# Self-attention inside a six-stage transformer program: score tiles of 32x64, one exponential per pair of batches, another order of the work around them

## The chip, the cores and the metric

The kernel is one program on one core of a Trainium2 chip. The metric is the device time of a run in microseconds (us). Three runs of the kernel before took 3310.77, 3310.79 and 3312.28 us; the median is 3310.79 us. "Within 0.2%" is 6.6 us of that.

## The reference

The input x is 8 batches of 64 rows of 512 features (512 rows in all). Six layers follow one another, each as x = x + layer(layernorm(x)): a cross attention with a GRU, a state space block, a convolution with attention and eight dense experts (stage 3), a cross attention over 1601 rows (stage 4), a causal self-attention with rotations (stage 5), and eight routed experts (stage 6). The change concerns the self-attention of stages 3 and 5, each over 64 rows of one batch, 16 heads of 32 features:

```python
# stage 3 (inside _L0_ffn_ref), after the convolution
scores = jnp.einsum('bhqd,bhkd->bhqk', q, k) / jnp.sqrt(jnp.float32(dh))
attn = jax.nn.softmax(scores, axis=-1)
ctx = jnp.einsum('bhqk,bhkd->bhqd', attn, v)
# stage 5 (_L1_attn_ref)
q = apply_rope(q, cos, sin)
k = apply_rope(k, cos, sin)
scores = jnp.einsum('bqhd,bkhd->bhqk', q, k) * SCALE
scores = jnp.where(causal[None, None], -1e+30, scores)
attn = jax.nn.softmax(scores, axis=-1)
out = jnp.einsum('bhqk,bkhd->bqhd', attn, v).reshape(B, S, D)
```

## The kernel before

Everything is FP32. Activations lie with features on 128 partitions: a tile [128, 4, 512] holds 4 chunks of 128 features (index c or g) by 512 rows. A chunk g holds four heads, head a of it on partitions 32a to 32a+31. Each engine has its own program, written by hand, and these programs meet through semaphores: `at.step(name)` counts, `wait_ge(*at.done(name))` waits. PSUM `PS` has eight banks of 512 columns; `bank_reader[k]` is the name of the step that last read bank k, and TensorE waits for it before it writes the bank again.

The attention (`attn_pe`, `attn_act`, `attn_dve`, `attn_pool`) works in four pairs of batches (`bp`, `NBP` = 4, 128 rows). For a pair:

- Scores (L1183): one matmul per chunk g gives all four heads at once, 128 query rows by 4 x 128 key columns. For this the keys are copied into a block-diagonal tile `KBD` (zero outside a head's 32 partitions), the first pair by VectorE (L1244, 4 copies), the other pairs by GpSimd (L1172). Half of the 128x128 scores of a head are between different batches and are masked away.
- `maxima` on VectorE, for each half q of 8 heads: scale and mask (L1253, 128x1024), maximum (L1257), sign (L1259).
- `exps` on ScalarE: 16 activations of 128x128 with a bias and an accumulated sum (L1225).
- Normalise on VectorE, for each half: reciprocal (L1271), multiply (L1273, 128x1024).
- `values` on TensorE: 16 transposes of the probabilities (L1195, T below) into banks 4 to 6, copied out by ScalarE (L1235), then 16 matmuls of 128x32 stationary values (L1204, O below) into bank 7, copied out by VectorE (`out`, L1263).

The order on VectorE is written out: maxima(0), maxima(1), then for bp = 0 to 3: normalise(bp), and from bp = 1 on out(bp-1) and maxima(bp+1). On TensorE: scores(0), scores(1), then values(bp) and scores(bp+2).

Ahead of it, in stage 3, come the linears for q, k (L296) and v (L1289, bias added by VectorE at L1297). In stage 5 come q, k, then four plus four rotation matmuls (L1796), each followed by three VectorE operations (L1802, L1803, L1805), then the v linear. After it comes the output linear (L296), the next norm and the experts. Both stages pass a mask tile.

Of the kernel before, what the change touches and what calls it, by code (L numbers as in the profile page):

```python
# [142 lines left out]
def build(nc, marks, new, t, stages=(1, 2, 3, 4, 5, 6)):  # L143
    ctx = ExitStack()
    with ctx:
# [71 lines left out]
        def bank(k, n=512):  # L217
            return PS[:, k, 0:n]
# [932 lines left out]
        KBD = [RB4[0], RB4[1]]  # L1151

# [3 lines left out]
        least = [misc[:, 0:H], misc[:, 16:16 + H]]  # L1156
# [3 lines left out]
        HALF_H = H // 2  # L1160

        def attn_pool(pool, at, tag, K, ready):
            for x in KBD:
                pool.memset(x[:, :, :], 0.0).then_inc(*at.step(f"{tag}.zero"))
            pool.wait_ge(*at.own())
            for due in at.last(*ready):
                pool.wait_ge(*due)
            for bp in range(1, NBP):
                if bp >= 2:
                    pool.wait_ge(*at.done(f"{tag}.S{bp - 2}"))  # L1170
                for a in range(G):
                    pool.tensor_copy(KBD[bp % 2][a * HD:(a + 1) * HD, :, a * P:(a + 1) * P],  # L1172
                                        K[a * HD:(a + 1) * HD, :, bp * P:(bp + 1) * P]).then_inc(*at.step(f"{tag}.kb{bp}"))

        def attn_pe(pe, at, tag, Q, V, ready):
            def scores(bp):
                pe.wait_ge(*at.done(f"{tag}.kb{bp}"))
                for g in range(KC):
                    if bp:
                        pe.wait_ge(*at.done(f"{tag}.masked{bp - 1}.{g // 2}"))  # L1180
                    elif bank_reader.get(g):
                        pe.wait_ge(*at.done(bank_reader[g]))
                    mm = pe.matmul(bank(g), Q[:, g, bp * P:(bp + 1) * P], KBD[bp % 2][:, g, :], start=True, stop=True)  # L1183
                    if g % 2:
                        mm.then_inc(*at.step(f"{tag}.S{bp}.{g // 2}"))
                at.same(f"{tag}.S{bp}")

            def values(bp):
                for g in range(KC):
                    pe.wait_ge(*at.done(f"{tag}.p{bp}.{g // 2}"))  # L1190
                    k = 4 + g % 3
# [5 lines left out]
                    bank_reader[k] = f"{tag}.T{bp}.{g}.out"
                if bank_reader.get(7):
                    pe.wait_ge(*at.done(bank_reader[7]))
                for g in range(KC):  # L1200
                    pe.wait_ge(*at.done(f"{tag}.T{bp}.{g}.out"))
                    for a in range(G):
                        h = G * g + a
                        mm = pe.matmul(PS[a * HD:(a + 1) * HD, 7, g * P:(g + 1) * P], V[:, bp, h * HD:(h + 1) * HD],  # L1204
                                          probsT[:, h, :], start=True, stop=True)
                mm.then_inc(*at.step(f"{tag}.O{bp}"))
                bank_reader[7] = f"{tag}.O{bp}.out"

            for due in at.last(*ready):
                pe.wait_ge(*due)  # L1210
            scores(0)
            scores(1)
            for bp in range(NBP):
                values(bp)
                if bp + 2 < NBP:
                    scores(bp + 2)
            for g in range(KC):
                bank_reader[g] = f"{tag}.masked{NBP - 1}.1"

        def attn_act(act, at, tag):  # L1220
            def exps(bp):
                for h in range(H):
                    if h % HALF_H == 0:
                        act.wait_ge(*at.done(f"{tag}.least{bp}.{h // HALF_H}"))
                    act.activation(probs[bp % 2][:, h, :], probs[bp % 2][:, h, :], ACT.Exp, bias=least[bp % 2][:, h:h + 1],  # L1225
                                   accum_out=sums[bp % 2][:, h:h + 1]).then_inc(*at.step(f"{tag}.exp{bp}.{h // HALF_H}"))
# [3 lines left out]
            for bp in range(NBP):  # L1230
                for g in range(KC):
                    act.wait_ge(*at.done(f"{tag}.T{bp}.{g}"))
                    if bp:
                        act.wait_ge(*at.done(f"{tag}.O{bp - 1}"))
                    act.activation(PT[:, g, :], bank(4 + g % 3), ACT.Copy).then_inc(*at.step(f"{tag}.T{bp}.{g}.out"))  # L1235
                if bp and bp + 1 < NBP:
                    exps(bp + 1)

        def attn_dve(dve, at, tag, K, ready, O, mask):
            dve.wait_ge(*at.done(f"{tag}.zero"))  # L1240
            for due in at.last(*ready):
                dve.wait_ge(*due)
            for a in range(G):
                dve.tensor_copy(KBD[0][a * HD:(a + 1) * HD, :, a * P:(a + 1) * P],  # L1244
                                K[a * HD:(a + 1) * HD, :, 0:P]).then_inc(*at.step(f"{tag}.kb0"))

            def maxima(bp):
                if bp >= 2:
                    dve.wait_ge(*at.done(f"{tag}.T{bp - 2}.3"))
                for q in (0, 1):  # L1250
                    dve.wait_ge(*at.done(f"{tag}.S{bp}.{q}"))
                    x, m = probs[bp % 2][:, q * HALF_H:(q + 1) * HALF_H, :], least[bp % 2][:, q * HALF_H:(q + 1) * HALF_H]
                    dve.scalar_tensor_tensor(out=x, in0=PS[:, 2 * q:2 * q + 2, :].rearrange("p g (a k) -> p (g a) k", k=P),  # L1253
                                                 scalar=HD ** -0.5, in1=mask.unsqueeze(1).broadcast_to([P, HALF_H, P]),
                                                 op0=ALU.mult, op1=ALU.add).then_inc(*at.step(f"{tag}.masked{bp}.{q}"))
# [3 lines left out]
                    dve.tensor_scalar(m, m, -1.0, None, ALU.mult).then_inc(*at.step(f"{tag}.least{bp}.{q}"))  # L1259
# [919 lines left out]
```

## Time and profile before

| what | value |
|---|---|
| median of three runs | 3310.79 us |
| profiled execution, its own time | 3310.42 us |
| its span in the trace | 3308.6 us |
| mean granted TensorE clock | 0.949 |
| busy: PE, DVE, ACT, POOL | 89%, 40%, 31%, 8% of the span |
| attention of stage 3, first scores to last output copy | about 1141 to 1192 us |
| attention of stage 5, the same | about 3017 to 3070 us |

A duration of a matmul record includes its way through the array, so records overlap: the step from one to the next is shorter than a record. A row of the timeline gives start, length, what it is, and in brackets how long the engine idled before and what ended that.

### The profile page before, as it was taken

To read this page: it belongs to the slowest core of one execution; us is meant where nothing else is said; L and a number is where in the kernel's file an instruction comes from. 1 tells how busy PE (TensorE), PEld (TensorE's weight loads), DVE (VectorE), ACT (ScalarE), POOL (GpSimd) and SP (SyncE) were. 2 spreads that over 40 slices of the span, in tenths; PEclk is the share of its full clock that TensorE was granted. 3 is DMA by queue.
4 is the path that set the end of the run, shared out by engine and by line. 5 is a ranking of instruction groups with operands and counts; after the bars stand their busy time and mean duration, and the time that the engine had idled before them with its cause. 6 is when DMAs were issued, how large, how long until landed. Compare 5 with 4: busy or idle time off the path is not lost.

```text
span 3308.6 us, 35885 instructions
## 1 busy us (share of the span) xinstructions
PE 2950.1 (89%) x14622; PEld 2016.9 (61%) x14622; DVE 1337.6 (40%) x2005; ACT 1025.8 (31%) x1717; POOL 268.0 (8%) x274
## 2 busy tenths in 40 slices
PE   7766889888878879999999988999999999988787
PEld 3324537345555347888888857778777877844432
DVE  3435454454842243333333352442443344245211
ACT  3223212224331234433434322422332333233200
POOL 1110120122010000000000002011011101000000
PEclk9887999999889978999999999999999999998899
DMA  8663693861011002222222221001100100021097
GB/s 358 263 241 130 241 412 122 352 267 72 1 52 63 38 13 102 101 93 97 101 89 101 93 78 42 23 20 42 42 23 20 42 23 20 23 108 39 26 419 304
DMA packets 62267, 388.74 MB, mean 117 GB/s; under 512 B 5696, under 2 KB 12096, under 8 KB 32704
## 3 DMA queue, kind: packets, MB, share of 16 engines
q1 hardware_dynamic: 26640, 190.57, 15.2%
q0 software_dynamic: 29024, 192.23, 14.8%
q10 hardware_dynamic: 6480, 4.20, 0.4%
q8 instruction: 91, 1.49, 0.2%
q14 instruction: 32, 0.26, 0.0%
HBM read 381.72 MB, written 5.24 MB: 117 GB/s over the span
## 4 chain that ended last, share of the span: by engine, by line
PE 76%; DVE 7%; DMA 6%; ACT 5%; issue 4%; POOL 2%; SPq 0%; DVEq 0%; POOLq 0%; ACTq 0%
PE PS L373 10%; PE PS L375 10%; PE PS L374 10%; PE PS L544 4%; PE PS L296 4%; PE PS L1571 4%; PE PS L519 3%; PE PS L1552 3%; PE PS L1535 3%; PE PS L1554 3%; PE PS L1553 3%; PE PS L1537 3%; PE PS L1536 3%; DMA PR<-in_ctxN 3%; DMA ring<-in_experts 2%
## 5 line engine op out<-in xcount | busy, mean ns | idle before, releaser
L373 PE MATMUL PS<-X_high,W_high 128*128 128x512 f32 x576 | 226.1, 392 | 27.6 <-POOL W_part L1029 27.6
L374 PE MATMUL PS<-X_low,W_high 128*128 128x512 f32 x576 | 225.6, 392 | 0.0
L375 PE MATMUL PS<-X_high,W_part 128*128 128x512 f32 x576 | 225.5, 391 | 0.0
L375 PE MATMUL PS<-H_high,W_part 128*128 128x512 f32 x576 | 224.4, 390 | 0.0
L374 PE MATMUL PS<-H_low,W_high 128*128 128x512 f32 x576 | 224.4, 390 | 0.0
L373 PE MATMUL PS<-H_high,W_high 128*128 128x512 f32 x576 | 224.4, 390 | 0.0
L1037 DVE TENSOR_TENSOR W_part<-ring,W_high 128x2048 fp32r<-128x2048 f32 x63 | 147.0, 2334 | 188.6 <-ACT W_high L1004 188.6
L1004 ACT ACTIVATE W_high<-ring 128x2048 fp32r<-128x2048 f32 x72 | 136.9, 1914 | 255.0 <-PE PS L375 255.0
L1735 DVE TENSOR_TENSOR RB<-PS,rows 128x512 f32<-128x512 f32 x104 | 71.9, 691 | 307.2 <-PE PS L1554 307.2
L1043 DVE TENSOR_TENSOR H_low<-T,H_high 128x512 fp32r<-128x512 f32 x144 | 99.7, 692 | 221.2 <-ACT H_high L1024 221.2
L1535 PE MATMUL PS<-C_high,W_part 128*128 128x384 f32 (+2 forms) x512 | 177.7, 347 | 4.9 <-DVE W_part L1707 4.9
L1665 ACT ACTIVATE RC<-PS,vec 128x384 f32<-128x384 f32 (+2 forms) x128 | 76.2, 595 | 326.9 <-PE PS L1537 326.9
L1537 PE MATMUL PS<-C_high,W_part 128*128 128x384 f32 (+2 forms) x512 | 176.5, 345 | 0.0
L1536 PE MATMUL PS<-C_low,W_part 128*128 128x384 f32 (+2 forms) x512 | 176.5, 345 | 0.0
L544 PE MATMUL PS<-RC,PTs 128*64 128x512 f32 x312 | 144.7, 622 | 31.1 <-DVE PTs L871 23.4
L1552 PE MATMUL PS<-W_part,C_high 128*128 128x512 f32 x416 | 164.9, 396 | 0.0
L1553 PE MATMUL PS<-W_part,C_high 128*128 128x512 f32 x416 | 162.3, 390 | 0.0
L1554 PE MATMUL PS<-W_part,C_low 128*128 128x512 f32 x416 | 162.3, 390 | 0.0
L519 PE MATMUL PS<-RA,PR 128*64 128x448 f32 (+1 forms) x384 | 145.3, 538 | 18.5 <-DMA RB<-in_ctxT 8.2
L1023 ACT ACTIVATE T<-PS,vec 128x512 f32<-128x512 f32 x144 | 99.2, 689 | 197.1 <-PE PS L375 187.4
L296 PE MATMUL PS<-T,ring 128*128 128x512 f32 x288 | 135.4, 633 | 20.9 <-DVE T L363 10.0
L519 PE MATMUL PS<-RB,PR 128*64 128x448 f32 (+1 forms) x384 | 145.5, 539 | 0.0
(314 smaller groups left out, 5804.4 us busy)
## 6 DMA issues: line engine op xcount, KB each, us to landing
ring<-in_experts SPq DMA_DIRECT2D x96, 1024.0 KB, 4.8
ring<-in_tiles SPq DMA_DIRECT2D x39, 1024.0 KB, 4.8
RA<-in_ctxT POOLq DMA_DIRECT2D x20, 1792.0 KB, 8.9
RA<-in_ctxT POOLq DMA_DIRECT2D x20, 1536.0 KB, 6.9
T<-in_ctxN POOLq DMA_DIRECT2D x24, 1024.0 KB, 13.7
RA<-in_experts SPq DMA_DIRECT2D x24, 1024.0 KB, 12.4
RC<-in_ctxN POOLq DMA_DIRECT2D x12, 1792.0 KB, 12.7
RB<-in_ctxT POOLq DMA_DIRECT2D x12, 1792.0 KB, 13.4
```

Of the source, the lines that this page charges most:

```text
L296: mm = pe.matmul(bank(k), wt(w)[:, c, oc * P:(oc + 1) * P], x[:, c, :], start=(a == 0 and c == 0), stop=(a == len(terms) - 1 and c == KC - 1))
L373: pe.matmul(ps, a, xh, start=start, stop=False)
L374: pe.matmul(ps, a, xl, start=False, stop=False)
L375: return pe.matmul(ps, b, xh, start=False, stop=stop)
L519: mm = pe.matmul(PS[u * S:(u + 1) * S, 2 * h + j, 0:w], QP[:, c, u * S:(u + 1) * S], CT1[u][h][:, c, j * w:(j + 1) * w], start=(c == 0), s ...
L544: mm = pe.matmul(PS[u * S:(u + 1) * S, 6, :], A_[:, m, u * S:(u + 1) * S], cn(u, m), start=(m == 0), stop=(m == MT - 1))
L1535: pe.matmul(bank(n % 4, w), wkh[:, c, f], CH[h][:, c, m], start=(c == 0), stop=False)
L1536: pe.matmul(bank(n % 4, w), wkh[:, c, f], CL[h][:, c, m], start=False, stop=False)
L1537: mm = pe.matmul(bank(n % 4, w), wkl[:, c, f], CH[h][:, c, m], start=False, stop=(c == KC - 1))
L1552: pe.matmul(bank(k), CH[h][:, c, m], wvh[:, c, :], start=(c == 0), stop=False)
L1553: pe.matmul(bank(k), CH[h][:, c, m], wvl[:, c, :], start=False, stop=False)
L1554: mm = pe.matmul(bank(k), CL[h][:, c, m], wvh[:, c, :], start=False, stop=(c == KC - 1))
```

## The change

Scores become 32 matmuls per pair, one for each head and each of the two batches (32 contraction rows, 64 query columns stationary, 64 key columns moving), written to bank a, columns 64g on. No block-diagonal keys are needed. `KBD` and its copies go; GpSimd now zeroes the two probability tiles instead, whose off-diagonal 64x64 blocks stay zero. Exponentials are taken in place in `raw5` (128 x 16 x 64) by one activation per pair; the maximum is subtracted by VectorE before, the sum is reduced by VectorE after. Stage 3 has no mask any more.

```diff
+        def scores_pe(pe, at, tag, Q, K, bp):
+            if bp:
+                pe.wait_ge(*at.done(f"{tag}.raw{bp - 1}"))
...
             for g in range(KC):
+                for a in range(G):
+                    r = slice(a * HD, (a + 1) * HD)
+                    for u in (0, 1):
+                        m = slice((2 * bp + u) * S, (2 * bp + u + 1) * S)
+                        mm = pe.matmul(PS[u * S:(u + 1) * S, a, g * S:(g + 1) * S], Q[r, g, m], K[r, g, m], start=True, stop=True)
+            mm.then_inc(*at.step(f"{tag}.S{bp}"))
...
+                act.wait_ge(*at.done(f"{tag}.sub{bp}"))
+                act.activation(raw5[bp % 2], raw5[bp % 2], ACT.Exp, scale=HD ** -0.5).then_inc(*at.step(f"{tag}.exp{bp}"))
...
             def maxima(bp):
...
+                if mask:
+                    dve.tensor_tensor(x.rearrange("p (a g) k -> p a (g k)", a=G), PS[:, 0:G, 0:KC * S],
+                                      causal.rearrange("p g k -> p (g k)").unsqueeze(1).broadcast_to([P, G, KC * S]), ALU.add).then_inc(*at.step(f"{tag}.raw{bp}"))
                     dve.wait_ge(*at.own())
                     dve.tensor_reduce(m, x, AX.X, ALU.max).then_inc(*at.step())
                     dve.wait_ge(*at.own())
+                    dve.tensor_tensor(x, x, m.unsqueeze(2).broadcast_to([P, H, S]), ALU.subtract).then_inc(*at.step(f"{tag}.sub{bp}"))
+                    return
+                dve.tensor_reduce(m.rearrange("p (a g) -> p a g", a=G), ps, AX.X, ALU.max).then_inc(*at.step())
+                dve.wait_ge(*at.own())
+                dve.tensor_tensor(x.rearrange("p (a g) k -> p a g k", a=G), ps,
+                                  m.rearrange("p (a g) -> p a g", a=G).unsqueeze(3).broadcast_to([P, G, KC, S]), ALU.subtract).then_inc(*at.step(f"{tag}.sub{bp}"))
+                at.same(f"{tag}.raw{bp}", f"{tag}.sub{bp}")
+
+            def normalise(bp):
+                x, sm = raw5[bp % 2], sums[bp % 2]
+                dve.wait_ge(*at.done(f"{tag}.exp{bp}"))
+                dve.tensor_reduce(sm, x, AX.X, ALU.add).then_inc(*at.step())
+                dve.wait_ge(*at.own())
+                dve.reciprocal(sm, sm).then_inc(*at.step())
...
+                for u in (0, 1):
+                    r = slice(u * S, (u + 1) * S)
+                    dve.tensor_tensor(probs[bp % 2][r, :, r], x[r, :, :], sm[r, :].unsqueeze(2).broadcast_to([S, H, S]), ALU.mult).then_inc(*at.step(f"{tag}.p{bp}"))
...
             maxima(0)
+            values(0, 2)
             maxima(1)
+            values(2, 4)
             for bp in range(NBP):
...
+                normalise(bp)
                 if bp:
                     out(bp - 1)
-                    if bp + 1 < NBP:
-                        maxima(bp + 1)
+                if bp + 2 < NBP:
+                    maxima(bp + 2)
             out(NBP - 1)
...
+            scores_pe(pe, at, "s3.at", Q3, K3, 0)
+            values_pe(pe, at, "s3.v", "s3.wv", X3, (4, 5, 6, 7), range(0, 2))
+            scores_pe(pe, at, "s3.at", Q3, K3, 1)
+            values_pe(pe, at, "s3.v", "s3.wv", X3, (4, 5, 6, 7), range(2, 4))
...
+            for c in range(KC):
+                linear_pe(pe, at, "s5.k", [("s5.wk", N5)], (4 + c,), (c,))
+                rotate_pe(pe, at, "s5.qr", Q5, "s5.q", (c,), 0)
+            for c in range(KC):
+                rotate_pe(pe, at, "s5.kr", K5, "s5.k", (c,), 4)
+                values_pe(pe, at, "s5.v", "s5.wv", N5, (0, 1, 2, 3), range(c, c + 1))
```

TensorE waits for `p{bp}` of both halves before the first transpose of a pair. In the kernel after, `values_of(bp)` stands for `values(bp)`, and `values(a, b)` inside `attn_dve` adds the bias to the v linear's tiles a to b-1 (in stage 5 they are all added ahead of the attention).

TensorE in stage 3, from the v linear to the last pair. T holds q, k, v; sq is the identity; RC and RA hold the two probability tiles. Before:

```order
L1289 MATMUL PS<-ring,T 128x512 x16
L1183 MATMUL PS<-RB,T 128x512 x8
L1195 MATMUL PS<-sq,RC 128x128 x16
L1204 MATMUL PS<-RC,T 32x128 x16
L1183 MATMUL PS<-RB,T 128x512 x4
L1195 MATMUL PS<-sq,RA 128x128 x16
```

With the change:

```order
L1179 MATMUL PS<-T 64x64 x32
L1282 MATMUL PS<-ring,T 128x512 x8
L1179 MATMUL PS<-T 64x64 x32
L1282 MATMUL PS<-ring,T 128x512 x8
L1192 MATMUL PS<-sq,RC 128x128 x16
L1201 MATMUL PS<-RC,T 32x128 x16
L1179 MATMUL PS<-T 64x64 x32
L1192 MATMUL PS<-sq,RA 128x128 x16
```

Both first score groups moved ahead of or between the v linear's tiles; a score group is 32 small matmuls where it was four.

VectorE in the same stage, from the first reciprocal on (RB holds `raw5` in the change). Before:

```order
L1271 RECIPROCAL misc<-misc 128x8
L1273 TENSOR_TENSOR RC<-RC,misc 128x1024
L1271 RECIPROCAL misc<-misc 128x8
L1273 TENSOR_TENSOR RC<-RC,misc 128x1024
L1271 RECIPROCAL misc<-misc 128x8
L1273 TENSOR_TENSOR RA<-RA,misc 128x1024
L1271 RECIPROCAL misc<-misc 128x8
L1273 TENSOR_TENSOR RA<-RA,misc 128x1024
L1263 COPY T<-PS 128x4x128
L1253 SCALAR_TENSOR_TENSOR RC<-PS,sq 128x1024
```

With the change:

```order
L1245 TENSOR_REDUCE misc<-RB 128x16
L1247 RECIPROCAL misc<-misc 128x16
L1255 TENSOR_TENSOR RC<-RB,misc 64x16x64 x2
L1236 TENSOR_REDUCE misc<-PS 128x16
L1238 TENSOR_TENSOR RB<-PS,misc 128x1024
L1245 TENSOR_REDUCE misc<-RB 128x16
L1247 RECIPROCAL misc<-misc 128x16
L1255 TENSOR_TENSOR RA<-RB,misc 64x16x64 x2
L1259 COPY T<-PS 128x4x128
L1236 TENSOR_REDUCE misc<-PS 128x16
```

The maxima of pair 2 (L1236, which read the scores of pair 2 from PSUM) now stand between the normalisation of pair 0 and that of pair 1; before, pair 1 was normalised first. Stage 5 has the same order with L1229, L1232 and L1234 in place of L1236 and L1238.

## Rows read from the trace of the kernel before

**Rows 1.** The page, busy time of each engine

```profile
PE 2950.1 (89%) x14622; PEld 2016.9 (61%) x14622; DVE 1337.6 (40%) x2005; ACT 1025.8 (31%) x1717; POOL 268.0 (8%) x274
```

**Rows 2.** Chain of waits in order of time, stage 5: start, length, what

```profile
3017.51 3.60 PE PS L1183 x4
3024.21 6.26 ACT RC L1225 x32
```

**Rows 3.** Timeline of PE, stage 3 attention: start, length, what, idle before

```profile
1155.74 2.82 PE L1195 MATMUL PS<-sq,RC 128*128 128x128 f32 x12 [6.03 <-DVE RC L1273]
1159.64 1.09 PE L1195 MATMUL PS<-sq,RC 128*128 128x128 f32 x4 [1.07 <-ACT RC L1235]
1160.66 1.94 PE L1204 MATMUL PS<-RC,T 128*32 128x128 f32 x32
1162.52 4.39 PE L1183 MATMUL PS<-RB,T 128*128 128x512 f32 x8
1166.75 2.01 PE L1195 MATMUL PS<-sq,RA 128*128 128x128 f32 x16
1168.68 1.25 PE L1204 MATMUL PS<-RC,T 128*32 128x128 f32 x32
1169.86 3.70 PE L1183 MATMUL PS<-RB,T 128*128 128x512 f32 x8
1185.03 1.97 PE L1195 MATMUL PS<-sq,RA 128*128 128x128 f32 x8 [4.47 <-DVE RA L1273]
```

**Rows 4.** Timeline of ACT and PE, stage 3, end of k and the v linear

```profile
1124.97 13.90 PE L1289 MATMUL PS<-ring,T 128*128 128x512 f32 x32
...
1125.18 0.69 ACT L1408 ACTIVATE T<-PS,vec 128x512 f32<-128x512 f32 x1 [2.75 <-PE PS L296]
```

**Rows 5.** Timeline of DVE, stage 3

```profile
1138.91 0.69 DVE L1297 TENSOR_TENSOR T<-PS,rows 128x512 f32<-128x512 f32 x1 [2.74 <-PE PS L1289]
...
1144.78 1.22 DVE L1257 TENSOR_REDUCE misc<-RC 128x8 f32<-128x1024 f32 x1
...
1154.23 0.20 DVE L1271 RECIPROCAL misc<-misc 128x8 f32<-128x8 f32 x1
1154.46 1.22 DVE L1273 TENSOR_TENSOR RC<-RC,misc 128x1024 f32<-128x1024 f32 x1
...
1191.74 0.69 DVE L1263 COPY T<-PS 128x512 f32<-128x512 f32 x1 [3.09 <-PE PS L1204]
```

**Rows 6.** Timeline of PE and DVE, stage 5: rotations, v linear, first transposes, last copy

```profile
3001.11 13.90 PE L1289 MATMUL PS<-ring,T 128*128 128x512 f32 x32
3033.36 2.82 PE L1195 MATMUL PS<-sq,RC 128*128 128x128 f32 x12 [6.03 <-DVE RC L1273]
...
3010.17 0.69 DVE L1805 TENSOR_TENSOR T<-T 128x512 f32<-128x512 f32 x1
...
3069.14 0.69 DVE L1263 COPY T<-PS 128x512 f32<-128x512 f32 x1 [3.02 <-PE PS L1204]
```

**Rows 7.** Windows: stretch, its length, PE, PEld, DVE, ACT, POOL busy, clock, DMA

```profile
1156.00:1163.00 7.00, 5.93 (x49) 4.75 (x49) 4.17 (x6) 5.05 (x20) 0.00 (x0) 0.50 0.01 2
1163.00:1170.00 7.00, 7.00 (x57) 4.00 (x57) 4.95 (x6) 2.62 (x8) 0.00 (x0) 0.93 0.00 1
...
1185.00:1192.00 7.00, 5.53 (x48) 4.45 (x48) 2.28 (x4) 5.10 (x14) 0.00 (x0) 0.55 0.00 0
...
3033.00:3040.00 7.00, 5.57 (x48) 4.53 (x48) 4.40 (x7) 5.66 (x24) 0.00 (x0) 0.50 0.00 0
```

**Rows 8.** Small tiles: matmuls and weight loads, timeline; L1204's forms, ns min/median/max

```profile
L1204 PE MATMUL PS<-RC,T x256: 272/421/424, 1160.7 to 3068.8; 128*32 128x128 f32 x128
...
2894.66 1.09 PE L1602 MATMUL PS<-PTs,RB 128*64 128x128 f32 x16
...
1168.68 0.59 PEld L1204 LDWEIGHTS PS<-RC,T 128*32 128x32 f32 x24 [0.17 <-issue]
...
2888.83 0.20 PEld L1571 LDWEIGHTS PS<-RC,T 32*64 32x64 f32 x8 [0.35 <-issue]
```

More of the change, by code:

```diff
@@ L1159, in build @@
         NBP = T // P
[L1160 to L1191, printed above, removed]
+        def attn_pool(pool, at, tag):
+            for k, x in enumerate(probs):
+                pool.memset(x, 0.0).then_inc(*at.step(f"{tag}.zero{k}"))
@@ L1197, in values @@
[L1197 to L1205, printed above, removed]
@@ new lines, in scores_pe, with values_of @@
+            mm.then_inc(*at.step(f"{tag}.S{bp}"))
+            if bp == NBP - 1:
+                bank_reader.update({k: f"{tag}.raw{bp}" for k in range(G)})
+        def values_of(pe, at, tag, V, bp):
+            for g in range(KC):
+                if g == 0:
+                    pe.wait_ge(*at.done(f"{tag}.p{bp}"))
+                k = 4 + g % 3
+                if bank_reader.get(k):
+                    pe.wait_ge(*at.done(bank_reader[k]))
+                for a in range(G):
+                    mm = pe.transpose(PS[:, k, a * P:(a + 1) * P], probs[bp % 2][:, G * a + g, :], C["ident"])
+                mm.then_inc(*at.step(f"{tag}.T{bp}.{g}"))
+                bank_reader[k] = f"{tag}.T{bp}.{g}.out"
+            if bank_reader.get(7):
+                pe.wait_ge(*at.done(bank_reader[7]))
+            for g in range(KC):
+                pe.wait_ge(*at.done(f"{tag}.T{bp}.{g}.out"))
+                for a in range(G):
+                    h = G * g + a
+                    mm = pe.matmul(PS[a * HD:(a + 1) * HD, 7, g * P:(g + 1) * P], V[:, bp, h * HD:(h + 1) * HD],
+                                      probsT[:, h, :], start=True, stop=True)
+            mm.then_inc(*at.step(f"{tag}.O{bp}"))
+            bank_reader[7] = f"{tag}.O{bp}.out"
@@ L1235, in attn_act, with attn_dve @@
                     act.activation(PT[:, g, :], bank(4 + g % 3), ACT.Copy).then_inc(*at.step(f"{tag}.T{bp}.{g}.out"))
[L1236 to L1245, printed above, removed]
-            def maxima(bp):
[L1248 to L1255, printed above, removed]
+                if bp + 2 < NBP:
+                    exps(bp + 2)
+        def attn_dve(dve, at, tag, O, mask, values):
+            def maxima(bp):
+                x, m = raw5[bp % 2], peak[bp % 2]
+                ps = PS[:, 0:G, 0:KC * S].rearrange("p a (g k) -> p a g k", k=S)
+                dve.wait_ge(*at.done(f"{tag}.S{bp}"))
+                if mask:
+                    dve.tensor_tensor(x.rearrange("p (a g) k -> p a (g k)", a=G), PS[:, 0:G, 0:KC * S],
+                                      causal.rearrange("p g k -> p (g k)").unsqueeze(1).broadcast_to([P, G, KC * S]), ALU.add).then_inc(*at.step(f"{tag}.raw{bp}"))
                     dve.wait_ge(*at.own())
@@ L1291, in values_pe, with values_dve @@
                 bank_reader[k] = f"{tag}.{tt}.out"
-            at.same(w + ".used", f"{tag}.3")
-        def values_dve(dve, at, tag, V, bias, banks):
-            for tt in range(T // P):
+            if tts[-1] == T // P - 1:
+                at.same(w + ".used", f"{tag}.3")
+        def values_dve(dve, at, tag, V, bias, banks, tts=range(T // P)):
+            for tt in tts:
                 dve.wait_ge(*at.done(f"{tag}.{tt}"))
@@ L1354, in s3_pool @@
             pool.memset(XPAD[:, :, :, S + 1:S + 2], 0.0).then_inc(*at.step("s3.pad"))
-            attn_pool(pool, at, "s3.at", K3, [f"s3.k.{c}.out" for c in range(KC)])
+            attn_pool(pool, at, "s3.at")
             with at.loop(pool, "s3.loop", E_) as i:
@@ L1788, in build, with rotate_pe @@
         trig = RC[:, 4200:4200 + 2 * T].rearrange("p (a s) -> p a s", a=2)
[L1790 to L1797 removed]
+        def rotate_pe(pe, at, tag, x, of, cs, k0):
+            for c in cs:
+                pe.wait_ge(*at.done(f"{of}.{c}.out"))
+                if bank_reader.get(k0 + c):
+                    pe.wait_ge(*at.done(bank_reader[k0 + c]))
+                pe.matmul(bank(k0 + c), C["rot"], x[:, c, :], start=True, stop=True).then_inc(*at.step(f"{tag}.{c}"))
+                bank_reader[k0 + c] = f"{tag}.{c}.out"
         def rotate_dve(dve, at, tag, x, tmp, banks):
```

84 lines of the change are left out of this document (32 added, 52 removed).

## The prediction

> **What bounds the kernel now.** I read the page first, then the chain of waits, then the timelines of TensorE and VectorE over the two attentions, then their clock. The page says that TensorE is busy 89% of the span [rows 1], but that is an average; the attentions are other stretches. There the chain runs through TensorE (a first score matmul), then through ScalarE's exponentials, 6.26 us for one pair [rows 2]. The timeline of stage 3 shows what this does to TensorE: it idles 6.03 us before the first transposes, 1.07 us within them and 4.47 us before those of pair 3 [rows 3]. So the attentions are bound by latency: TensorE, VectorE and ScalarE hand a pair on, and each waits. Because of the idling the granted clock is 0.50 in the seven microseconds from 1156 and 0.93 in the next seven, 0.55 from 1185 and 0.50 from 3033 [rows 7]. What counts is the length of the chain per pair. From the first transposes to the last output copy stage 3 takes 1191.74 - 1155.74 = 36.0 us [rows 3, 5] and stage 5 takes 3069.14 - 3033.36 = 35.8 us [rows 6].
>
> **What stays.** Transposes and value matmuls (I call them V, for a pair) are as before. At the low clock V took 1162.52 - 1155.74 = 6.78 us, of which 1.07 was a wait for ScalarE, which was still in exponentials; that wait goes, so 5.7 us. At the full clock it took 1169.86 - 1166.75 = 3.1 us [rows 3].
>
> **What goes at no gain or a small one.** GpSimd's key copies are off the chain for pairs 1 to 3 except for pair 1's second start; the zeroing of two tiles replaces the zeroing of two others of the same size. Exponentials fall from 6.2 us a pair to one activation of 1024 elements. At most 1.4 us (twice the 0.69 of a 512-element activation [rows 4]) and beside VectorE's next work, so I count them as nothing: VectorE has the next maxima or a reduction of another pair to do in that time. If that cover fails, the price is 1.4 us per round.
>
> **VectorE per pair.** Every 128x1024 operation takes 1.22, a dependent one starts 1.25 after it, and a reciprocal takes 0.23 with its wait [rows 5]. Maxima in stage 3: reduce, subtract, 2.5 us. In stage 5: add the mask, reduce, subtract, 3.7 us. Normalise: reduce, reciprocal, two multiplies of 64 partitions by 1024, which I cost as 128 partitions since the free size is the same: 1.25 + 0.23 + 1.15 + 1.22 = 3.85 us. So VectorE has 6.35 us or 7.55 us of work per pair where it had about 8; it gains little, although half the scores are gone.
>
> **Scores (S).** No row has a 32x64 tile with 64 moving columns. Bounds: from below, eight weight loads of 32x64 tiles stand in 0.20 us, about 10 ns each, and 24 loads of 128x32 tiles in 0.59, 21 ns each [rows 8]. From above, the 128x64 tiles go at (1.09 - 0.27)/15 = 54 ns a record [rows 8], and twice that at half clock. The value matmuls (128x32, 128 moving columns) lie between: (1.25 - 0.27)/31 = 32 ns a record at full clock, (1.94 - 0.42)/31 = 49 at the low one [rows 3, 8]. They are nearest, but each tile streams twice as many columns. A pair has 64 records. I take 27 ns at full clock, halfway from 21 to 32, and 38 when cold, halfway from 27 to 49: S = 1.7 + 0.27 = 2.0 us and 2.4 + 0.42 = 2.8 us. Ends: 0.9 to 3.75 us at full clock, 1.1 to 7.4 us at the low one.
>
> **Stage 3.** TensorE waits for the last key chunk, out at 1125.18 + 0.69 = 1125.9 [rows 4]. Then S(0), the v linear's 13.9 us [rows 4] with S(1) in its middle: 1125.95 + 1.7 + 13.9 + 1.7 = 1143.3. The bias of the last tile takes 0.6, and now normalise(0) starts, because the written order puts it behind values(2, 4): 1143.9 + 3.85 = 1147.8 for the first transposes. Before: 1155.74 [rows 3]. So 7.9 us are won here.
>
> Then something is given back. On VectorE maxima(2) stands ahead of normalise(1). It needs the scores of pair 2, which TensorE makes after V(0). So one round is serial: V(0), S(2), maxima(2), normalise(1), and only then V(1); the same for pair 3. During VectorE's 6.35 us TensorE has nothing to do. It idled 6.03 and 4.47 us before, and after both the records are those of the low clock [rows 3, 7], so I take V and S cold in each round: 5.7 + 2.8 + 2.5 + 3.85 + 0.1 for semaphores = 14.95 us. The distances before were 11.0 us from the first to the second transposes (1166.75) [rows 3], and 36.0 in all. Two rounds end at 1177.7. V(2) is 5.7; normalise(3) and an output copy, 4.5 us, hide beside it. V(3) follows at once, partly at the full clock: between 3.1 and 5.7 I take 4.2. Last copy at 1187.6, against 1191.74 [rows 5]: **4.1 us faster**.
>
> **Stage 5.** The k linear, eight rotations and the v linear are the same TensorE work without a wait, so the v linear still ends at 3001.11 + 13.9 = 3015.0 [rows 6]. VectorE's rotations ended at 3010.9 before [rows 6]; now the last rotation matmul comes at 3011.5, one v tile from the end, so they end at 3013.4 and the four biases at 3015.9. The key copies that stood there are gone. S(0) to 3017.95, maxima(0) 3.7, maxima(1) 3.7, normalise(0) 3.85: first transposes at 3029.3 where it was 3033.36 [rows 6], 4.1 won. A round is 1.25 longer than in stage 3: 16.2 us. Two rounds, then 5.7 + 4.2: last copy at 3071.6, against 3069.14 [rows 6]: **2.5 us slower**. Moving the rotations wins nothing, since VectorE and TensorE were both done at nearly the same moment already.
>
> **Sum.** -4.1 + 2.5 = -1.6 us. Both ends are followed by the output linear and a norm on the chain, so it all reaches the end. The profiled execution took 3310.42 us, so it would be 3308.8; the median of the runs, 3310.79, is 0.4 above, so 3309.2 us. A measurement of this kernel can tell about 0.2%, 6.6 us, from no change.
>
> **The rivals.**
>
> 1. The clock stays up in the rounds. Then V is 3.1 and S 2.0, a round 11.55 or 12.8 us. Stage 3 ends at 1147.8 + 23.1 + 6.2 = 1177.1 (14.6 faster), stage 5 at 3029.3 + 25.6 + 6.2 = 3061.1 (8.0 faster): 3288 us. For it: a stretch at 0.93 between the idles [rows 7]. Against it: 0.50 and 0.55 after idles no longer than those to come. 12%.
> 2. The tiles really run side by side and S costs about 1 us. That takes 1.1 off S(0) and S(1) in stage 3 and S(0) in stage 5, and 1.7 off four later ones, 10.1 us: 3299 us. For it: the 10 ns loads of 32x64 tiles [rows 8]. Against it: nothing in the trace shows matmuls of such tiles as short as these. 20%.
> 3. Slower: loads and matmuls of a batch's two column tiles do not overlap, so a record takes the step of the 128x64 tile, 54 ns, and twice it at half clock. S is 3.75 and 7.4 us. Stage 3 pays 2 x 1.75 + 2 x 4.6 = 12.7, stage 5 1.75 + 1.25 + 2 x 4.6 = 12.2 more: 3334 us. If the clock comes back in the middle of S (after 8 us it did, within the scores at 1162.52, whose eight matmul records took 4.39 instead of 3.70 [rows 3]), S is 4.9 and the time 3324 us. It decides from a cold S of about 4.3 us, 60 ns a record. Against it: 24 loads of 128x32 tiles went in 0.59 us while matmuls ran [rows 8]. 15%. The Trainium skill has a rule for this (TensorE: Matmul & The Clock Gate, Packing small matmuls): weight loads overlap with running matmuls only if the row group differs, and here each row group has two matmuls in a row. The trace's 24 loads share all rows and do overlap, so it does not bear the rule out.
> 4. The operations that VectorE now does (reduction straight from four banks, half-partition multiplies) cost more than the rows say: 1 us a round would be some 6 us. 4%.
>
> **How the numbers follow.** 49% for my case, whose own range is 3303 to 3316 us (V(3), the clock's return and S by some tenths each). Its lower end and rivals 1 and 2 give 34% for faster by over 0.2%; rivals 3 and 4 give 19% for slower; 47% lies within 0.2%. The range that leaves out 2 in 10 reaches from near rival 1, 3291, to the milder form of rival 3, 3326.
>
> **What would show it.** In the profile after: first transposes near 1148 and 3029; the distance from the first to the second transposes 15 and 16 us; TensorE idle some 6 and 7.6 us before the second and third; ScalarE's exponentials of about 1.1 us waited for by nobody; S as one group of 64 records in 2 to 3 us; clock near 0.5 after each idle. I am wrong if TensorE does not wait for the multiplies of pair 1 (then the order on VectorE does not matter), if S is outside 1 to 4 us, or if the second transposes start at full clock.

## The result, and the profile after

The changed kernel takes 3298.22 us (median of 6 runs, 3296.19 to 3299.69) against 3311.35 us (median of 6, 3310.05 to 3314.25). The ratio is 0.9959, with a 95% interval from 0.9947 to 0.9971: 13 us less, about 0.4%. Forecast were 3309.2 us, with a range from 3291 to 3326, and "within 0.2%" as the likeliest outcome. The time is in the range; the outcome is the one that had 34%. It lies outside 3303 to 3316 us, the range of my main case.

The page of the kernel after, its span and busy times (they answer to [rows 1]):

```profile
span 3296.5 us, 36447 instructions
PE 2928.5 (89%) x15070; PEld 2011.3 (61%) x15070; DVE 1325.8 (40%) x1969; ACT 986.5 (30%) x1469; POOL 253.8 (8%) x250
```

The averages say little: the shares of PE and DVE are the same. ScalarE's busy time is 39 us less, and the time fell by 12. The difference must be looked for in the attentions.

Stage 3, timeline of PE in the kernel after: start, length, what, idle before. L1179 are the scores, L1282 the v linear, L1192 transposes, L1201 value matmuls (they answer to [rows 3]):

```profile
1128.54 0.90 PE L1179 MATMUL PS<-T 32*64 32x64 f32 x64 [0.87 <-ACT T L1410]
1129.37 7.13 PE L1282 MATMUL PS<-ring,T 128*128 128x512 f32 x16
1136.44 0.91 PE L1179 MATMUL PS<-T 32*64 32x64 f32 x64
1137.28 7.13 PE L1282 MATMUL PS<-ring,T 128*128 128x512 f32 x16
1149.12 3.42 PE L1192 MATMUL PS<-sq,RC 128*128 128x128 f32 x16 [4.70 <-DVE RC L1255]
1152.47 1.23 PE L1201 MATMUL PS<-RC,T 128*32 128x128 f32 x32
1153.63 0.91 PE L1179 MATMUL PS<-T 32*64 32x64 f32 x64
1161.04 3.68 PE L1192 MATMUL PS<-sq,RA 128*128 128x128 f32 x16 [6.50 <-DVE RA L1255]
1164.65 1.94 PE L1201 MATMUL PS<-RC,T 128*32 128x128 f32 x32
1166.51 0.91 PE L1179 MATMUL PS<-T 32*64 32x64 f32 x64
1173.92 3.32 PE L1192 MATMUL PS<-sq,RC 128*128 128x128 f32 x16 [6.49 <-DVE RC L1255]
...
1178.69 2.00 PE L1192 MATMUL PS<-sq,RA 128*128 128x128 f32 x16 [0.34 <-DVE RA L1255]
```

A pair's 64 score records take 0.91 us. And the round is serial, as forecast: TensorE idles 6.50 and 6.49 us before pairs 1 and 2. Timeline of VectorE beside it, from the last bias (L1291) on, and ScalarE's exponential of pair 2 (they answer to [rows 5]):

```profile
1144.45 0.69 DVE L1291 TENSOR_TENSOR T<-PS,rows 128x512 f32<-128x512 f32 x1 [2.74 <-PE PS L1282]
1145.06 1.21 DVE L1245 TENSOR_REDUCE misc<-RB 128x16 f32<-128x1024 f32 x1
1146.30 0.25 DVE L1247 RECIPROCAL misc<-misc 128x16 f32<-128x16 f32 x1
1146.59 2.47 DVE L1255 TENSOR_TENSOR RC<-RB,misc 64x1024 f32<-64x1024 f32 x2
1154.58 1.23 DVE L1236 TENSOR_REDUCE misc<-PS 128x16 f32<-128x1024 f32 x1 [5.52 <-PE PS L1179]
1155.84 1.22 DVE L1238 TENSOR_TENSOR RB<-PS,misc 128x1024 f32<-128x1024 f32 x1
1156.98 1.21 DVE L1245 TENSOR_REDUCE misc<-RB 128x16 f32<-128x1024 f32 x1
...
1158.51 2.47 DVE L1255 TENSOR_TENSOR RA<-RB,misc 64x1024 f32<-64x1024 f32 x2
...
1181.99 0.69 DVE L1259 COPY T<-PS 128x512 f32<-128x512 f32 x1 [2.63 <-PE PS L1201]
```

```profile
1157.10 1.06 ACT L1209 ACTIVATE RB<-RB 128x1024 f32<-128x1024 f32 x1 [3.93 <-DVE RB L1238]
```

VectorE is free from 1149.1 on, with pair 1's exponentials done since 1141. It waits 5.52 us for the scores of pair 2, and normalises pair 1 only behind their maxima. Operations that read four banks of PSUM take 1.22 to 1.23 us, and two of 64 partitions 2.47, near the 1.22 and 2.37 that I had costed.

Stage 5, timeline of PE (answers to [rows 6]):

```profile
3008.54 0.90 PE L1179 MATMUL PS<-T 32*64 32x64 f32 x64 [1.16 <-DVE T L1291]
3010.76 0.91 PE L1179 MATMUL PS<-T 32*64 32x64 f32 x64 [1.32 <-DVE RB L1229]
3020.84 3.67 PE L1192 MATMUL PS<-sq,RC 128*128 128x128 f32 x16 [9.17 <-DVE RC L1255]
3024.45 1.94 PE L1201 MATMUL PS<-RC,T 128*32 128x128 f32 x32
3026.31 1.09 PE L1179 MATMUL PS<-T 32*64 32x64 f32 x64
3035.15 3.68 PE L1192 MATMUL PS<-sq,RA 128*128 128x128 f32 x16 [7.75 <-DVE RA L1255]
```

Windows over transposes and value matmuls of pairs 0 and 1 in stage 3 and of pair 0 in stage 5, columns as in [rows 7]:

```profile
1149.00:1153.60 4.60, 4.49 (x48) 3.96 (x48) 0.06 (x1) 2.39 (x4) 0.00 (x0) 0.63 0.02 4
...
1161.00:1166.50 5.50, 5.46 (x48) 4.66 (x48) 0.69 (x1) 2.39 (x4) 0.00 (x0) 0.50 0.02 3
```

```profile
3020.80:3026.30 5.50, 5.46 (x48) 4.66 (x48) 0.00 (x0) 2.39 (x4) 0.00 (x0) 0.50 0.00 0
```

The clock was granted at 0.50 in two of the three, and returned within the first (0.63 over the stretch), where V took 4.5 us instead of 5.5. Between the waits it came back: the scores S(2) and S(3) of stage 3 and S(3) of stage 5 ran at 1.00, and S(2) of stage 5, the one of 1.09 us, at 0.79.

To compare kernels I use two lengths that depend little on what happened earlier in the program. Stage 3: from the start of ScalarE's last key chunk to the start of the last output copy. Stage 5: from the start of the last residual of stage 4 to the first matmul of the output linear. The rest is the span less both. The runs come from four sets, each with the kernel before beside it (medians 3311.35 for the first, then 3313.99, 3313.09 and 3311.85 us); each ratio below is against the kernel before of its own set, and medians of different sets can be compared only within about 3 us. The profiled execution is one of the runs, seldom the median one.

| kernel (profiled execution) | stage 3 | stage 5 | rest | median of runs |
|---|---|---|---|---|
| before | 66.6 | 119.6 | 3122.4 | 3311.35 |
| after | 54.3 | 115.8 | 3126.5 | 3298.22 |
| after, once more | 54.3 | 115.7 | 3126.3 | 3298.57 |
| v linear ahead | 57.7 | 115.7 | 3127.2 | 3301.98 |
| rotations back | 54.3 | 113.0 | 3124.7 | 3293.90 |
| 16 exponentials | 54.3 | 115.7 | 3126.6 | 3298.37 |
| old order | 48.8 | 109.3 | 3126.5 | 3284.52 |
| tile by tile | 60.6 | 122.3 | 3122.7 | 3308.74 |
| filler | 52.0 | 112.0 | 3123.8 | 3291.73 |
| two and two | 45.9 | 105.8 | 3124.6 | 3277.81 |
| all | 43.4 | 102.7 | 3125.3 | 3271.72 |
| old order, 16 sums | 54.1 | 115.7 | 3126.5 | 3299.01 |
| two and two, rotations back | 45.9 | 104.9 | 3127.3 | 3278.10 |
| column halves | 55.6 | 115.9 | 3123.3 | 3296.67 |

The two stages became 12.3 and 3.9 us shorter, 16.1 together. Most of it lies ahead of the first transposes: they come 9.2 us earlier in stage 3 and 5.0 in stage 5. From there to the last copy stage 3 takes 32.9 us instead of 36.0, and stage 5 takes 36.9 instead of 35.8.

The rest lies between 3122.4 and 3127.3 us in kernels whose code does not differ there. Of the 4 us more in the changed kernel about half repeats: from the last copy of stage 3 to the last residual of stage 4 the kernel before took 1758.5 us, and the two executions of the changed kernel 1760.7 and 1760.8. Part of that is TensorE at the low clock for longer in the same work, here over the first 6.2 us of the experts' matmuls, before and after:

```profile
1255.70:1261.90 6.20, 6.16 (x19) 4.96 (x20) 2.05 (x1) 1.16 (x2) 0.00 (x0) 0.69 0.00 0
```

```profile
1246.00:1252.20 6.20, 6.20 (x15) 4.87 (x16) 1.98 (x1) 0.51 (x1) 0.00 (x0) 0.53 0.00 0
```

The granted clock is 0.69 and 0.53. So a change in a stage can go with another clock well behind it; what sets this was not found. The other half is not shown to come from the change: until the last key chunk of stage 3 the kernel before took 1125.2 us and the two executions of the changed kernel 1127.7 and 1126.7, so this part moves by 1 us from one execution to the next.

### The profile page after: what moved, and what is told of

The parts are those of the page before. It is cut to its first block, busy times and chain, and to the rows that moved or that the text cites. A ratio compares the mean times of both kernels' runs of the same rounds, so it can differ in the third digit from the quotient of the medians.

```text
span 3296.5 us, 36447 instructions
## 1 busy us (share of the span) xinstructions
PE 2928.5 (89%) x15070; PEld 2011.3 (61%) x15070; DVE 1325.8 (40%) x1969; ACT 986.5 (30%) x1469; POOL 253.8 (8%) x250
## 4 chain that ended last, share of the span: by engine, by line
PE 71%; issue 10%; DVE 7%; DMA 6%; ACT 4%; POOL 2%; SPq 0%; DVEq 0%; POOLq 0%; ACTq 0%
PE PS L374 9%; PE PS L376 9%; PE PS L375 9%; PE PS L545 4%; PE PS L1572 4%; PE PS L520 3%; PE PS L1553 3%; PE PS L1536 3%; PE PS L1555 3%; PE PS L1554 3%; PE PS L1538 3%; PE PS L1537 3%; PE PS L297 3%; DMA PR<-in_ctxN 3%; PE PS L1589 2%
## 6 DMA issues: line engine op xcount, KB each, us to landing
RA<-in_experts SPq DMA_DIRECT2D x24, 1024.0 KB, 11.7
```

## The experiments

The theory after the result: the round is serial, as forecast, but its score term is small (eight tiles run side by side), and V costs what the clock makes it cost. The rivals: the exponentials, the moved linears or rotations, or a bound by VectorE's sum of work.

**The changed kernel once more.** 

> The changed kernel once more, beside the experiments of its batch. From the last key chunk of stage 3 to the last output copy about 54.3 us, from the last residual of stage 4 to the last output copy of stage 5 about 115 us; 3298 us within 3 us. The theory (cheap score tiles on a serial round) and its rivals expect the same.

Measured 3298.57 us (ratio 0.9955, 0.9938 to 0.9971), both lengths within 0.1 us of the first execution. Stage lengths repeat far better than whole runs do, so tenths are read from them and only microseconds from runs.

**The v linear ahead of the scores again.**

```diff
+            values_pe(pe, at, "s3.v", "s3.wv", X3, (4, 5, 6, 7), range(0, 4))
...
             scores_pe(pe, at, "s3.at", Q3, K3, 0)
-            values_pe(pe, at, "s3.v", "s3.wv", X3, (4, 5, 6, 7), range(0, 2))
             scores_pe(pe, at, "s3.at", Q3, K3, 1)
-            values_pe(pe, at, "s3.v", "s3.wv", X3, (4, 5, 6, 7), range(2, 4))
...
+            values(0, 4)
             maxima(0)
-            values(0, 2)
             maxima(1)
-            values(2, 4)
```

> Stage 3 only: the whole v linear goes back ahead of the scores. Theory: maxima(0), maxima(1) and normalise(0) then follow the v linear one after the other instead of beside it. First transposes 3.0 us later (v ends at the same time, then 0.9 scores, 2.5 + 0.9 + 2.5 + 3.85), everything behind them unchanged: +3 us. Rival (the gain of stage 3 comes mostly from the interleaved v linear): +8 us or more.

First transposes 3.1 us later (24.5 after the key chunk, 21.4 in the changed kernel), the stage 3.4 us longer, 3301.98 us (ratio 0.9962, 0.9948 to 0.9976). So the interleaved v linear is worth about 3 of stage 3's 12.3 us. The other 6 us that the first transposes come earlier were not taken apart between the key copies that went, the shorter scores and the smaller work on VectorE; the exponentials are not among them, as the run with sixteen and their sums has its first transposes at 21.4 too.

**The rotations back.**

```diff
-            for c in range(KC):
-                linear_pe(pe, at, "s5.k", [("s5.wk", N5)], (4 + c,), (c,))
-                rotate_pe(pe, at, "s5.qr", Q5, "s5.q", (c,), 0)
-            for c in range(KC):
-                rotate_pe(pe, at, "s5.kr", K5, "s5.k", (c,), 4)
-                values_pe(pe, at, "s5.v", "s5.wv", N5, (0, 1, 2, 3), range(c, c + 1))
+            linear_pe(pe, at, "s5.k", [("s5.wk", N5)], (4, 5, 6, 7), range(KC))
+            rotate_pe(pe, at, "s5.qr", Q5, "s5.q", range(KC), 0)
+            rotate_pe(pe, at, "s5.kr", K5, "s5.k", range(KC), 4)
+            values_pe(pe, at, "s5.v", "s5.wv", N5, (0, 1, 2, 3))
```

> Stage 5 only: the rotation matmuls go back behind both linears, all eight in a row. Theory: the end of the v linear sets the start of the scores either way, so the first scores come 0.4 us earlier or later, the time within 1 us. Rival (the moved rotations bring stage 5's gain of 4 us): +4 us.

3293.90 us (ratio 0.9941, 0.9925 to 0.9958). Stage 5 became 2.8 us shorter, outside my "within 1 us" and against the rival's sign. The timeline of PE tells two things apart (compare 5.47 and 5.40 us from transposes to scores of pairs 0 and 1 in the changed kernel):

```profile
3018.96 3.29 PE L1192 MATMUL PS<-sq,RC 128*128 128x128 f32 x16 [9.17 <-DVE RC L1255]
3022.18 1.21 PE L1201 MATMUL PS<-RC,T 128*32 128x128 f32 x32
3023.32 0.91 PE L1179 MATMUL PS<-T 32*64 32x64 f32 x64
3031.98 3.60 PE L1192 MATMUL PS<-sq,RA 128*128 128x128 f32 x16 [7.75 <-DVE RA L1255]
3035.51 1.18 PE L1201 MATMUL PS<-RC,T 128*32 128x128 f32 x32
3036.62 0.91 PE L1179 MATMUL PS<-T 32*64 32x64 f32 x64
```

First transposes come 0.3 us earlier relative to the last residual of stage 4. The other 2.3 us are three V within which the clock rose earlier: 4.36, 4.64 and 4.76 us where they took 5.47, 5.40 and 5.20 (granted 0.68 and 0.63 over the first two), behind the same idles of 9.17 and 7.75 us. The moved rotations gain nothing. Whether the early rise belongs to this order or to chance was tried once more below.

**Sixteen exponentials.**

```diff
-                act.activation(raw5[bp % 2], raw5[bp % 2], ACT.Exp, scale=HD ** -0.5).then_inc(*at.step(f"{tag}.exp{bp}"))
+                for h in range(H):
+                    act.activation(raw5[bp % 2][:, h, :], raw5[bp % 2][:, h, :], ACT.Exp, scale=HD ** -0.5).then_inc(*at.step(f"{tag}.exp{bp}"))
```

> Sixteen activations of 128x64 per pair in place of one of 128x1024 (no accumulated sum). About 0.32 us each, 5.1 us per pair instead of 1.06. Theory: in this order ScalarE has that time, since maxima(bp+2) is followed by the normalisation of the other pair; stage 3 +0.5 us, stage 5 +1.8 us (normalise(0) waits for exp(0)). Rival (the single exponential is the gain): +4 us a round, +16 us or more.

3298.37 us (ratio 0.9951, 0.9935 to 0.9968), both stages as in the changed kernel to 0.1 us. The sixteen took 2.44 us, 0.15 each, half of what I had expected, in part because no sum is read out (with it they start every 0.24 us, below):

```profile
3012.11 2.44 ACT L1210 ACTIVATE RB<-RB 128x64 f32<-128x64 f32 x16 [21.87 <-DVE RB L1235]
```

So in the changed order 1.4 us more per pair on ScalarE cost nothing. This run cannot rule on the 5 us that I had meant to add. A later one adds 2.8 us a pair, but in the old order; in the changed order a longer time on ScalarE was not tried.

**The old order on VectorE and ScalarE.**

```diff
-                if bp + 2 < NBP:
-                    exps(bp + 2)
+                if bp and bp + 1 < NBP:
+                    exps(bp + 1)
...
-                if bp + 2 < NBP:
-                    maxima(bp + 2)
+                if bp and bp + 1 < NBP:
+                    maxima(bp + 1)
```

> The changed kernel with the order on VectorE and ScalarE as in the kernel before: normalise(0), normalise(1), output, maxima(2), normalise(2), output, maxima(3), normalise(3); ScalarE copies pair 1's transposes ahead of exp(2). Theory (the round is serial because maxima(2) stands ahead of normalise(1)): V(1) follows S(2) at once; from first transposes to last copy 27.4 us in stage 3 (32.9 now) and 31 us in stage 5 (36.9 now), about -12 us in all. Rival (the round is bound by VectorE's sum of work, whatever the order): 0.

3284.52 us (ratio 0.9917, 0.9901 to 0.9934). From first transposes to last copy 27.43 us in stage 3, forecast 27.4; stage 5 became 6.4 us shorter. Timeline of PE, stage 3:

```profile
1152.91 1.21 PE L1201 MATMUL PS<-RC,T 128*32 128x128 f32 x32
1154.05 0.91 PE L1179 MATMUL PS<-T 32*64 32x64 f32 x64
1154.89 2.00 PE L1192 MATMUL PS<-sq,RA 128*128 128x128 f32 x16
```

Pair 1's transposes follow the scores of pair 2 at once and at the full clock. The order that came with the change costs 11.9 us of the two stages (5.4 and 6.4) and 14 us of the medians, nearly as much as the whole change brings. VectorE does the same work in both, so its sum is not the bound.

**Tile by tile.**

```diff
-            for g in range(KC):
-                for a in range(G):
+            for a in range(G):
+                for u in (0, 1):
                     r = slice(a * HD, (a + 1) * HD)
-                    for u in (0, 1):
+                    for g in range(KC):
```

> The same 32 score matmuls per pair, ordered so that the four of one 32x64 tile stand in a row (loops a, u, g). Theory (S is 0.9 us because eight tiles run side by side, and S is on the chain): a tile takes 53 ns a record (64 columns, two passes, 2.4 GHz), so S becomes about 3.6 us; +2.7 us for each of the four S of stage 3 and three of stage 5, +1.2 for the fourth, about +20 us. Rival 1 (issue alone sets 0.9 us): S stays, 0. Rival 2 (S is off the chain): S grows, time stays.

3308.74 us (ratio 0.9989, 0.9979 to 0.9998): 10 us slower than the changed kernel, stage 3 by 6.4, stage 5 by 6.6 us, so 13 by the stages. A score group:

```profile
1136.39 2.69 PE L1179 MATMUL PS<-T 32*64 32x64 f32 x64
```

2.69 us, so (2.69 - 0.22)/63 = 39 ns a record instead of (0.91 - 0.22)/63 = 11; 0.22 is the 217 ns of one record. The sign and the place are as expected, the size is half to two thirds. My 53 ns a record was too much. Both rivals fall: the scores are on the chain, and it is the order of the tiles, not the issue alone, that makes them cheap.

**Filler.**

```diff
+        def warm(pe, at, n):
+            pe.wait_ge(*at.done(bank_reader[5]))
+            for _ in range(n):
+                pe.matmul(bank(5), C["ident"], row("iota_slot", D), start=True, stop=True)
```

> Idle TensorE does unused FP32 matmuls of 128x512 into bank 5: 3 before the first transposes of stage 3, 4 after S(2) and S(3); 8 and 5 in stage 5. They leave 2 to 3 us of idling. Theory (V takes 5.5 us only because the clock is at 1.2 GHz after idles of 5 to 9 us): the transposes run at 2.4 GHz, V 3.1 us; stage 3 -5.4 us, stage 5 -6.9 us, about -12 us. Rival (V is bound by the copies out of PSUM): V stays, 0; if the fillers overrun the wait, slower.

3291.73 us (ratio 0.9939, 0.9922 to 0.9956), stage 3 2.3 us and stage 5 3.7 us shorter, half of what I expected. In stage 3:

```profile
1146.64 3.42 PE L1197 MATMUL PS<-sq,RC 128*128 128x128 f32 x16 [2.13 <-DVE RC L1260]
...
1158.56 2.00 PE L1197 MATMUL PS<-sq,RA 128*128 128x128 f32 x16 [2.87 <-DVE RA L1260]
...
1169.14 2.00 PE L1197 MATMUL PS<-sq,RC 128*128 128x128 f32 x16 [2.87 <-DVE RC L1260]
```

V(1) and V(2) ran at 2.4 GHz (2.00 us of transposes), the transposes of V(0) did not in spite of fillers (granted 0.55). And V(2)'s gain went into waiting for normalise(3), 1.53 us. The 2.3 us of stage 3 are thus V(1), 3.17 us instead of 5.47. In stage 5 V(0) took 3.17 us instead of 5.47 and V(1) 4.51 instead of 5.40. So V is bound by the clock and not by the copies out of PSUM. V(0) and V(1) are on the chain, V(2) only in part.

**Two and two.**

```diff
-                if bp + 2 < NBP:
-                    exps(bp + 2)
+                if bp == 1:
+                    exps(2)
+                    exps(3)
...
+            normalise(0)
+            normalise(1)
+            out(0)
+            maxima(2)
+            out(1)
+            maxima(3)
+            normalise(2)
+            normalise(3)
+            out(2)
+            out(3)
```

> Order on VectorE: normalise(0), normalise(1), output 0, maxima(2), output 1, maxima(3), normalise(2), normalise(3), outputs; ScalarE: exp(2) and exp(3) between the copies of pairs 1 and 2. Theory of the serial round: from first transposes to last copy 25.7 us in stage 3 (32.9) and 28 us in stage 5 (36.9), about -16 us, and better than both kernels. Rival (VectorE's sum bounds it): 0.

3277.81 us (ratio 0.9896, 0.9879 to 0.9912). First transposes to last copy 24.45 us in stage 3 (25.7 expected), stage 5 10.0 us shorter. TensorE now has one idle of 6.50 us, where the changed kernel has two:

```profile
1165.41 3.68 PE L1192 MATMUL PS<-sq,RC 128*128 128x128 f32 x16 [6.50 <-DVE RC L1256]
```

**All together:** two and two, rotations back, and more fillers (5 and 7 in stage 3, 8 and 8 in stage 5).

> The order of two and two, the rotations behind both linears again, and unused matmuls while TensorE would idle: 5 and 7 in stage 3, 8 and 8 in stage 5. Theory (what is left is the low clock of V(0) and V(2)): stage 3's last copy 1.3 + 2.1 us earlier than with the order alone, stage 5's 2.4 + 2.0 + 0.3 us: about 8 us below its 3277.8 us, 3270. Rival (as before the first transposes of stage 3 in the filler run, which stayed at 1.2 GHz): only half, 3274; worse if a filler overruns.

3271.72 us (ratio 0.9878, 0.9862 to 0.9894), 26 us below the changed kernel and 6 below two and two. V(0) to V(3) of both stages ran at the full clock, two of them in stage 3:

```profile
1149.78 2.00 PE L1197 MATMUL PS<-sq,RC 128*128 128x128 f32 x16 [0.41 <-DVE RC L1261]
...
1164.39 2.00 PE L1197 MATMUL PS<-sq,RC 128*128 128x128 f32 x16 [0.29 <-DVE RC L1261]
```

What stays between first transposes and last copy in stage 3 is 22 us.

**Old order with sixteen exponentials and their sums.** As the old order, and

```diff
-                act.activation(raw5[bp % 2], raw5[bp % 2], ACT.Exp, scale=HD ** -0.5).then_inc(*at.step(f"{tag}.exp{bp}"))
+                for h in range(H):
+                    act.activation(raw5[bp % 2][:, h, :], raw5[bp % 2][:, h, :], ACT.Exp, scale=HD ** -0.5,
+                                   accum_out=misc[:, 128 + 16 * bp + h:129 + 16 * bp + h]).then_inc(*at.step(f"{tag}.exp{bp}"))
```

> The old order on VectorE and ScalarE with the new tiles, and sixteen activations of 128x64 per pair, each with an accumulated sum that nobody reads: about 0.32 us each, 5.1 us a pair. Theory: the single exponential is worth nothing in the changed order, but 4 us a round in the old one, where normalise(bp+1) waits for it: stage 3 +8 us, stage 5 +9.6 us over the old order's 3284.5, so about 3302. Rival (ScalarE hides there too): 3285.

3299.01 us (ratio 0.9961, 0.9947 to 0.9975), 14.5 us over the old order by the medians and 11.7 by the stages: stage 3 by 5.3, stage 5 by 6.4 us. ScalarE's groups over the whole execution:

```profile
L1210 ACT ACTIVATE RB<-RB 128x64 f32<-128x64 f32 x128 | 30.6, 242 | 29.4 <-DVE RB L1236 23.2 <-DVE RB L1240 6.3
L1210 ACT ACTIVATION_READ_ACCUMULATOR RB<-RB 128x1 f32 x128 | 24.0, 188 | 0.0
```

One and its sum start every 0.24 us, so 3.84 us a pair instead of 1.06. In the old order the single exponential is worth about 12 us. The changed order has a wait for TensorE and VectorE in that place, and there 1.4 us more on ScalarE did not show.

**Two and two with the rotations back.** 

> The order of two and two with the rotations behind both linears, no fillers. Theory (going back with the rotations wins 0.3 us; the other 2.5 us of that run came from a clock that happened to rise earlier in V(0) and V(1)): first transposes of stage 5 0.3 us earlier, the last copy 0.3 us earlier or where the clock rises early up to 2.5. Rival (the moved rotations themselves cost 2.7 us): 2.7 us earlier.

3278.10 us (ratio 0.9898, 0.9882 to 0.9915). First transposes again 0.3 us earlier, stage 5 0.9 us shorter than two and two. The clock rose early in V(0) (4.35 us instead of 5.47), as in the other kernel with the rotations back, and late in V(2) (5.47 instead of 5.00). So the 2.3 us belong to when the clock rises, and beside a move of 0.3 us that moment went in either direction; what sets it was not settled.

**Column halves.**

```diff
-            for g in range(KC):
+            for u, g in ((u, g) for u in (0, 1) for g in range(KC)):
                 for a in range(G):
                     r = slice(a * HD, (a + 1) * HD)
-                    for u in (0, 1):
+                    if True:
```

> The 32 score matmuls with the column half outermost (loops u, g, a), so that neighbours lie in different row groups and four tiles are in turn at a time. Theory (a tile needs about 38 ns a record as in the tile-by-tile run, and four or eight in turn hide that): S stays 0.9 us, the time that of the changed kernel. Rival (two matmuls of one row group in a row cost something, as the row group rule says): S falls below 0.9. Rival 2 (eight tiles in turn are needed): S about 1.5 us, +4 us.

```profile
1134.88 1.06 PE L1179 MATMUL PS<-T 32*64 32x64 f32 x64
```

1.06 us, 3296.67 us (ratio 0.9958, 0.9941 to 0.9974), both stages within 1.3 us of the changed kernel's. Four tiles in turn are nearly as good as eight, and S did not fall when neighbours lie in different row groups. The run changes both at once (eight tiles in turn to four, and the row groups of neighbours), so what each is worth alone is not shown. In the changed kernel, with two matmuls of one row group in a row, the 64 weight loads of S(2) stand in 0.78 us and begin together with its matmuls:

```profile
1153.63 0.78 PEld L1179 LDWEIGHTS PS<-T 32*64 32x64 f32 x64 [0.20 <-issue]
```

## Why the prediction was right and wrong

- **Right: the serial round.** Maxima(2) ahead of normalise(1) was read from the order alone. TensorE idles 6.5 and 7.75 us there, and the old order takes 11.9 us out of the two stages. But the rounds were shorter than forecast: from the first to the second transposes 11.9 and 14.3 us, forecast 15 and 16.2.
- **Right: VectorE's terms.** Maxima and normalise in stage 3 were forecast at 6.35 us; from 1154.58 to the end at 1160.98 they took 6.40. First transposes 21.4 us after the key chunk, forecast 22.6; in stage 5 78.1 after the last residual, forecast 79.0.
- **Wrong in size: the scores.** I took 2.0 us at the full clock and 2.8 in a round. Measured 0.91, and 1.09 in the one that began at the low clock. That is below 1 us, one of my own signs that I am wrong. The step that failed is "They are nearest, but each tile streams twice as many columns": I took a value between two rows of 128-row tiles, where the load rows of 32x64 tiles (10 ns) were the right ones; a record takes 11 ns. I also took S as cold in every round, and it was at 1.00 in three of the four. In stage 3 this is 1.7 us ahead of the first transposes and 3.8 in the rounds, in stage 5 1.1 and 3.6: 10.2 of the 14.5 us by which both stages ended earlier than forecast. The rule of TensorEngine Tiling, Instruction Overhead, in the Trainium skill, 60 cycles for each matmul however small, I had counted per record. Counted per matmul, 25 ns at 2.4 GHz for each of 32, it gives an estimated 0.8 us of starts, and the trace has 0.91 - 0.22 = 0.69 us.
- **Wrong in size: V.** 5.7 and 4.2 us were too long. V(0) of stage 3 took 4.5, the others 5.4 to 5.5, the last two together 8.1 and 8.5 where I had 9.9. That is 5.2 us. Small terms elsewhere were 0.9 us too short, most of them ahead of the first transposes.
- **Wrong in sign: stage 5.** Forecast 2.5 us slower, it became 3.9 us faster, by the same two terms.
- **Rival 2** (S about 1 us, 3299 us) is what happened. That it comes within 0.9 us of the median is partly luck: the stages ended 4.3 us earlier than it says, and the rest of the program, which I took as unchanged, took some 3 to 4 us more. **Rival 1** did not happen: the clock was at 0.50 in V(1), though up in S behind it. **Rival 3** did not. Its row group rule (TensorE: Matmul & The Clock Gate, Packing small matmuls, in the Trainium skill) lets a load run beside matmuls only if the row group differs, though the same section also names the background weight buffer as a way. The 64 loads in 0.78 us beside their matmuls do not bear out the first part, and no run here tells of the second. The order with neighbours in different row groups was slower, 1.06 against 0.91 us, but it also has fewer tiles in turn. **Rival 4** did not: the shapes cost what their free size says.
- **Right: exponentials counted as nothing.** In this order, yes. That they are worth 11.7 us of the stages in the old one I had not seen, since I priced each part only in the order that the change brings.

## What to carry to other kernels

When a change alters both the pieces and their order, price each: here the pieces brought 28 us of the two stages and the new order took 12 back, and the order of two and two with the clock held up brings the kernel to 3271.7. Look for an operation that makes its engine wait for another one while work that is ready stands behind it, as maxima(2) did ahead of normalise(1), and put the ready work in front. And for tiles of another shape take the price from the row that has that shape, even if it shows only the loads.

## What the runs showed of the hardware

- In groups of 32 FP32 matmuls of 32x64 tiles with 64 moving columns, at the full clock, a record starts every 11 ns on average when eight tiles take turns, every 13 with four ((1.06 - 0.22)/63), and every 39 when one tile has its four in a row.
- The clock returned at different points of nearly the same sequence: V(0) in stage 5 took 5.47 us, or 4.36 when the rotations stood elsewhere and it came 0.3 us earlier. With an idle of 2.13 us before them the transposes of V(0) of stage 3 ran mostly at the low clock (granted 0.55), with idles of 2.87 us V(1) and V(2) at the full one. So a filler's effect cannot be read from the idle it leaves alone.
- An activation of 128x64 starts every 0.15 us, with an accumulated sum every 0.24.
